# Two token-choice layers: product order, transposition banks, bias on TensorE, output stored by batch

## What is computed

```python
x = x + _L1_ffn_ref(_layernorm(x), router_w, router_b, expert_w, expert_b)

def _L1_ffn_ref(x, router_w, router_b, expert_w, expert_b):
    k = int(bs * C / NUM_EXPERTS)                 # 2048 / 16 = 128 tokens for each expert
    xf = x.reshape(bs, h)
    S = jax.nn.softmax(xf @ router_w + router_b, axis=-1)
    G, idx = jax.lax.top_k(S.T, k)                # each expert takes its 128 best tokens
    tokens = xf[idx]
    out = jnp.einsum('ekh,hd->ekd', tokens, expert_w) + expert_b
    weighted = G[..., None] * out
    y = jnp.zeros((bs, h)).at[idx.reshape(-1)].add(weighted.reshape(-1, h))
    return y.reshape(b, s, h)
```

## Time and profile before

| | us |
|---|---|
| median of 3 runs (lowest to highest) | 3072.86 (3069.28 to 3079.09) |
| the profiled execution, its own time | 3071.74 |
| its span in the profile | 3070.0 |
| PE busy | 2791.3 (91%) |
| DVE busy | 1616.8 (53%) |
| POOL busy | 996.4 (32%) |
| ACT busy | 844.4 (28%) |
| mean granted clock of PE, of full speed | 0.924 |

### The profile page before, as it was taken

How to read it: one execution, slowest core, us unless ns; L and a number is a source line. 1 busy time by engine, 2 the same in 40 slices (tenths; PEclk the granted TensorE clock), 3 DMA queues, 4 the chain that set the end, 5 groups by cost and what they waited for, 6 DMA issues and landing times. The chain is left out here.

```text
span 3070.0 us, 45793 instructions
## 1 busy us (share of the span) xinstructions
PE 2791.3 (91%) x15592; PEld 1943.7 (63%) x15592; DVE 1616.8 (53%) x4517; ACT 844.4 (28%) x1372; POOL 996.4 (32%) x1109
## 2 busy tenths in 40 slices
PE   7999999999999999999978999999999658888876
PEld 3434448887656556788867888888887533443444
DVE  4566645555655647455534333333344566555556
ACT  2343344443111101344432222222222002222210
POOL 0000027766544435577741122222221011212211
PEclk8999999999999999999989999999998558888875
DMA  3000020000000000200000000000000000000000
GB/s 142 1 0 0 0 103 1 0 0 0 1 0 0 0 0 0 83 0 0 0 14 1 15 15 15 15 1 15 15 1 1 24 0 1 1 1 0 1 0 28
DMA packets 6289, 37.96 MB, mean 12 GB/s; under 512 B 273, under 2 KB 4369, under 8 KB 4497
## 3 DMA queue, kind: packets, MB, share of 16 engines
q1 hardware_dynamic: 6160, 36.34, 3.0%
HBM read 34.24 MB, written 2.10 MB: 12 GB/s over the span
## 5 line engine op out<-in xcount | busy, mean ns | idle before, releaser
L603 PE MATMUL banks<-back 32*128 32x512 f32 (+3 forms) x1088 | 363.9, 599 | 31.5 <-DVE back L613 22.3
L365 PE MATMUL banks<-moe_parts 128*128 128x512 f32 x1536 | 366.9, 394 | 16.8 <-POOL moe_parts L471 10.3
L830 ACT ACTIVATE back<-banks 128x1024 f32<-128x1024 f32 (+3 forms) x256 | 217.1, 863 | 457.8 <-PE banks L724 457.5
L365 PEld LDWEIGHTS banks<-moe_parts 128*128 128x128 f32 x1536 | 286.2, 190 | 79.7 <-issue 22.4
L1449 PE MATMUL banks<-lin_parts 128*128 128x512 f32 x1152 | 309.1, 414 | 19.3 <-DVE lin_parts L1705 15.5
L1640 DVE TENSOR_TENSOR ffn_pack<-banks,back 128x512 f32<-128x512 f32 x128 | 88.5, 692 | 393.7 <-PE banks L1462 393.6
L1449 PEld LDWEIGHTS banks<-lin_parts 128*128 128x128 f32 x1152 | 213.2, 194 | 78.2 <-issue 31.2
L724 PE MATMUL banks<-back 32*128 32x512 f32 (+3 forms) x1024 | 239.4, 577 | 20.2 <-DVE back L846 12.8
L603 PEld LDWEIGHTS banks<-back 32*128 32x128 f32 x1088 | 134.2, 197 | 186.3 <-DVE back L617 77.9
L1770 POOL TENSOR_TENSOR ffn_pack<-ffn_pack 128x256 f32<-128x256 f32 x112 | 82.6, 738 | 456.9 <-ACT ffn_pack L1603 455.5
L617 DVE TENSOR_REDUCE back<-banks 128x1 f32<-128x512 f32 x272 | 176.5, 687 | 80.3 <-PE banks L603 75.6
(11 more groups left out here) (234 smaller groups left out, 5154.6 us busy)
## 6 DMA issues: line engine op xcount, KB each, us to landing
back<-p_raw SPq DMA_DIRECT2D x8, 1024.0 KB, 4.8
back<-p SPq DMA_DIRECT2D x1, 7696.0 KB, 21.2
ffn_pack<-ffn SPq DMA_DIRECT2D x1, 6144.0 KB, 26.8
back<-p SPq DMA_DIRECT2D x1, 5152.0 KB, 15.1
back<-p SPq DMA_DIRECT2D x2, 1792.0 KB, 8.2
out<-x SPq DMA_DIRECT2D x1, 2048.0 KB, 7.5
x<-x_in SPq DMA_DIRECT2D x1, 1536.0 KB, 12.7
small_pack<-small SPq DMA_DIRECT2D x1, 619.0 KB, 5.0
```

What stands on the lines that cost most here:

```text
L365: mm = nc.tensor.matmul(bank[:], up[:, n % 2, a, which, kd, :], xp[:, b, kd, :], start=((a, b, kd) == (0, 0, 0)), stop=((a, b, kd) == (1, ...
L603: nc.tensor.matmul(bank[:, 0:n], qs[head_rows[j], hg, qi * P:(qi + 1) * P], ks[head_rows[j], hg, 0:n], start=True, stop=True).then_inc(D.f ...
L830: nc.scalar.activation(pt[:, (kt % 2) * 2 + pair, :, q0:T], two[:, :, q0:T], ACT.Exp, scale=0.25).then_inc(A.free.s, 2)
```

## The change

The layer's order on PE becomes: router of batch 0; the four products of batch 0; transpositions of batches 1 and 2; router of batch 1; transposition of batch 3; products 4 and 5; routers of batches 2 and 3; products 6 and 7; then the transposed scores. The remaining eight products follow the first eight counts. Ring S gets a second pair of banks. ACT copies two banks of y before the transposed batches, and a third before the softmax. The expert bias, which POOL added, is written into a bank of y by a matmul of the identity with the broadcast bias (512 columns), on which the two products then accumulate. In the last layer DVE signals after each batch of x, and SP stores that batch with a DMA of its own; the last block only waits.

```diff
-    S.take([c.psum[2]])
+    S.take([c.psum[1], c.psum[2]])
...
+    EARLY = 2 * NT
+
     def after_count(u):
 
-        return range(0, 2) if u < 0 else range(u + 2, u + 3) if u + 2 < B * NT else ()
+        return range(EARLY + u, EARLY + u + 1) if EARLY + u < B * NT else ()
...
+                if i % 2 == 0:
+                    nc.tensor.matmul(bank[:].rearrange("p (a d) -> p a d", a=2), c.ident[:],
+                                     eb.unsqueeze(1).to_broadcast([P, 2, DM]), start=True, stop=False,
+                                     skip_group_check=True)
                 for kd in range(KD):
                     mm = nc.tensor.matmul(bank[:, (i % 2) * DM:(i % 2 + 1) * DM], xt_of[b][:, kd, i * P:(i + 1) * P],
-                                          ew[:, kd, :], start=(kd == 0), stop=(kd == KD - 1))
+                                          ew[:, kd, :], start=False, stop=(kd == KD - 1), skip_group_check=True)
...
             router(0)
-            for b in range(1, B):
-                turn(b)
-                router(b)
-            for n in after_count(-1):
+            for n in range(NT):
+                product(n)
+            turn(1)
+            turn(2)
+            router(1)
+            turn(3)
+            for n in range(NT, NT + 2):
+                product(n)
+            router(2)
+            router(3)
+            for n in range(NT + 2, EARLY):
                 product(n)
...
+            keep_y(0)
+            keep_y(1)
+            for b in range(1, B):
+                keep_turned(b)
+            keep_y(2)
             act.wait_ge(c.lg_ready.s, c.lg_ready.at(0, 1))
             nc.scalar.activation(tiles, tiles, ACT.Exp).then_inc(c.ex_ready.s, 1)
-            for n in range(B * NT // 2):
+            for n in range(3, B * NT // 2):
                 keep_y(n)
...
-            dve.wait_ge(c.y_ready.s, c.y_ready.at(0, B * NT // 2))
+            dve.wait_ge(O.free.s, O.released(0, "y", B - 1, 1))
             for b in range(B):
                 for i in range(NT):
                     n = b * NT + i
                     ins = nc.vector.scalar_tensor_tensor(out=c.x[:, b, i, :], in0=y[:, b, i, :],
                                                          scalar=co[:, n // 2, n % 2:n % 2 + 1],
                                                          in1=c.x[:, b, i, :], op0=ALU.mult, op1=ALU.add)
-            link(ins)
+                ins.then_inc(c.mixed.s, 1)
+            dve.wait_ge(c.mixed.s, c.mixed.at(0, B))
...
-        @block.gpsimd
-        def _(pool):
-            pool.wait_ge(c.s_small.s, 16)
-            for n in range(B * NT // 2):
-                b, h = n // 2, n % 2
-                pool.wait_ge(O.free.s, O.released(0, "y", b, h))
-                ys = y[:, b, 2 * h:2 * h + 2, :]
-                nc.gpsimd.tensor_tensor(ys, ys, eb.unsqueeze(1).to_broadcast([P, 2, DM]), ALU.add)\
-                    .then_inc(c.y_ready.s, 1)
...
+        def store(sp):
+            for b in range(B):
+                sp.wait_ge(c.mixed.s, c.mixed.at(0, b + 1))
+                sp.dma_start(out_dram[:, b], c.x[:, b]).then_inc(c.s_out.s, 16)
+
...
-            (ATTENTION, [(choice_layer, load_p7), (mla_layer, nothing), (choice_layer, nothing)]),
+            (ATTENTION, [(choice_layer, load_p7), (mla_layer, nothing), (choice_layer, store)]),
...
-                sp.dma_start(out_dram, c.x[:]).then_inc(c.s_out.s, 16)
-                sp.wait_ge(c.s_out.s, 16)
+                sp.wait_ge(c.s_out.s, 16 * B)
```

More of the change, by code:

```diff
@@ L1862, in choice_layer @@
     D.take(c.banks[0:2])
-    S.take([c.psum[2]])
+    S.take([c.psum[1], c.psum[2]])
     O.take(c.banks[6:8])
     D.open(B + 1 + STEPS + 2)
-    S.open(B - 1)
+    S.open(B - 1, whole=False)
     O.open(B * NT // 2)
@@ L1871, in choice_layer @@
     c.s_ready.open(1)
-    c.y_ready.open(B * NT // 2)
+    c.mixed.open(B)
     c.sum_ready.open(STEPS + 3)
-    c.ve.open(14 + 4 + 2 * STEPS - 1 + 1 + 5)
+    c.ve.open(14 + 4 + 2 * STEPS - 1 + 1 + 4)
     xt_of = [c.xt] + [xts[:, b] for b in range(B - 1)]
     xn_of = [None, c.xn, xn2, c.xn]
+    EARLY = 2 * NT
     def after_count(u):
-        return range(0, 2) if u < 0 else range(u + 2, u + 3) if u + 2 < B * NT else ()
+        return range(EARLY + u, EARLY + u + 1) if EARLY + u < B * NT else ()
     with nc.Block() as block:
@@ L1956, in _, with keep_turned @@
             nc.scalar.activation(warm, c.ident[:, 0:1], ACT.Exp)
-            for b in range(1, B):
+            def keep_turned(b):
                 act.wait_ge(S.full.s, S.may_read(0))
@@ L2081, in _ @@
             loads(sp)
-    for k in (D, S, O, c.xn_ready, c.lg_ready, c.ex_ready, c.s_ready, c.y_ready, c.sum_ready, c.ve):
+    for k in (D, S, O, c.xn_ready, c.lg_ready, c.ex_ready, c.s_ready, c.mixed, c.sum_ready, c.ve):
         k.close(1)
@@ L2297, in program @@
         c.s_ready = Count(sem("s_ready"))
-        c.y_ready = Count(sem("y_ready"))
+        c.mixed = Count(sem("batch_mixed"))
         n1, nf, n3, n5, n7 = (a.shape[1] for a in (p1, ffn, p3, p5, p7))
```

## The result

The changed kernel took 3035.04 us (median of 4 runs, 3029.85 to 3042.10), the kernel before 3071.07 beside it (4 runs): ratio 0.9897, 95% interval 0.9872 to 0.9923. The profiled spans are 3070.0 and 3039.6, 30.4 us apart; the mean granted clock went from 0.924 to 0.939.

What follows compares the result with a forecast made beforehand. In the two token-choice layers, 89.5 us each, the chain hardly leaves PE and DVE, with PE mostly at half clock. Per layer -7 + 1 - 4.5 = -10.5, twice -21, store -5: -26, giving 3046 us, range 3033 to 3059.

Steps and rivals of the forecast that it cites:

- Stretch A: Layer start to last router, 28.9 us before: filling PE's idle time and closing gaps gains 7 us; 8.2 at full clock.
- Stretch B: Last router to transposed scores, 4.6 us before: 0.7 us gained at full clock, 1.8 lost at half; 1 lost taken.
- Stretch C: Fifteen threshold steps, 43.8 us before: 4.9 us gained without POOL's additions, bias now on PE; 4.5 gained taken.
- Stretch D: Ties, coefficients and 16 additions to x, 12.1 us before: same instructions, so zero change.
- The store: Behind the last layer: four pieces, one after each four additions, gain 4.2 to 5.2 us; 5 taken.
- The sum: Whole program: 10.5 us gained per layer, 21 for two, 5 at the store, 26 in all.
- Half clock only in the steps: Rival, threshold steps: the clock stays down after the last two routers, gaining only 12 us, 3060; 13%.
- Half clock throughout: Rival, whole layer: PE's clock falls in batch 0's first bank and never returns, slower than before, 3087; 3%.
- Stores in series: Rival, program end: each piece starts only when the one before has landed, 2.6 us later than now, 3053 or 3054; 8%.
- L2034 not cured: Rival, threshold steps: the 0.86 us multiplication is long for a reason other than POOL, 4.9 us not gained, 3056; 3%.
- signs of being wrong: Clock 0.50 in the first 20 us; early steps of 4 us; stores landing 4 us apart; PE idle before a router.

Runs made afterwards that it cites:

- e6: The changed kernel without products before the last router, the rest behind the counts; layers 75.56 and 76.30 us, against 74.80 and 77.14 with the change.
- e2: The changed kernel with the expert bias back on POOL and no identity matmul on PE; layers 84.28 and 84.73 us.
- e7: The kernel before without POOL's bias additions and nothing in their place; layers 84.56 and 84.58 us, against 89.48 and 89.49 before.
- e3: The changed kernel with the single store of before; from the last addition to the end of the span 8.6 us instead of 3.4.
- e1: The kernel before with only the bias moved from POOL to PE through the identity; layers 84.80 and 84.96 us, against 89.48 and 89.49 before.

## Why the prediction was right, and where it was off

The time fell inside the range, and for the reasons given in the main; some sizes and one reason were off. That it lies inside owes something to luck too: the layers gained 6 us more than forecast, and 4.1 of that were given back where the prediction had put nothing.

**Stretch A.** Taken: 7 us. Worked out at full clock: 8.2. Measured: 8.5 and 7.8. The clock was full in the ladder but for the last routers, and the ladder took 11.84 where 11.4 were worked out. The term was set too low because I stepped down from the full-clock sum without a row for it. The reason, "this stretch now begins with 20 such passes", is not shown: e6 has none of them there and reaches A = 18.9 and 21.5. Nor was the clock up in them throughout: it was 0.50 over 2962 to 2964, and the two banks took 7.1 us where 5.4 were worked out, which just fits into the 7.26. And "DVE's normalisation, which starts the ladder at S + 9.3, is not touched" holds only because the bias leaves POOL in the same change: in e2 the early copies of y put POOL's additions into that normalisation, and A gained 2.3 to 2.8 instead of 8. I had priced POOL's leaving in the steps alone; it is the order's condition too.

**Stretch B.** Both of its cases came, one in each layer: -0.64 where -0.7 was worked out at full clock, +1.54 where +1.8 was at half. The +1 taken was meant for both.

**Stretch C.** The 7 x 0.70 = 4.9 were right to 0.01 us (e7). "One late count (1.6) before the clock is back, six steps shorter by 0.2" was right in kind and off in size: the late step took 3.49 and 2.91, 0.87 and 0.29 beyond 2.62, and eight and seven steps that had been longer were 2.42. (The 3.0 for fifteen such steps counted the first, which took 2.42 before.) Measured -5.5 and -6.0, taken -4.5.

**Stretch D** was 12.16 in both layers, as before: zero, as said.

**The store.** Taken 5, measured 5.2 (e3). The pieces did not follow each other: each lands 3.0 us after its issue, and the next is issued 1.6 us after it. By the Trainium skill's "SBUF — State Buffer", section "The DMA setup-cost knee", one large transfer was the better form; for a result that becomes ready piece by piece at the end of the program, the measured end (3.4 us behind the last addition, against 8.6) decides otherwise.

**The sum.** Layers: -21 forecast, -27.0 measured. The rest of the program was costed at nothing; it took 4.1 more in the latent attention and 2.2 less ahead of layer 1. The second is no effect of the change: that start lay between 2400.6 and 2413.2 in the fourteen profiles, of kernels that do the same up to there. Such a scatter is larger than any single term of the sum, which is why the experiments were read by stretches. By medians the gain is 36 us where 27 were forecast; the runs of either kernel differ by 12 us and more.

**The rivals.** Half clock only in the steps fell: 1.00 over 2996 to 2998, steps of 2.42. Half clock throughout fell: 1.00 in the ladder. Stores in series fell (3.0 us each, issued 1.6 apart). L2034 not cured fell: no such operation over 0.2 us. Of the signs of being wrong one did appear, a clock of 0.50 in the first 20 us: it cost nothing, since it lay in the time in which PE had idled and the ladder still began at S + 9.25.

## What to carry to other kernels

Take a side engine's work off its engine before moving producers earlier: an addition on POOL that had cost 0.7 us in a step fell into DVE's normalisation when its input came early, and took back 5 to 6 us of 8. Where PE waits and its clock halves, an order without gaps can be worth more than less work; but two edits that both close gaps need not add up, so test each without the other. A final store that follows the work piece by piece left only its last piece to wait for. And where a stage with a changing clock follows, measure a gain behind that stage.

## What was not expected of the hardware

- A POOL fill of 0.95 us that only writes doesn't hold DVE's two-input operation (0.16 us inside it); beside a POOL addition of 1.09 us such an operation took 0.86 to 0.95, and a one-input operation on 128x12 int32 (L164) 1.09.
- With 14 more passes of PE among a layer's counts, most steps took 2.42 us instead of 2.63 (e1 against e7).
- Two transposition groups in a row at half clock were followed by full clock in e6 (router 1.71), and in the last layer of e2 by 8 us more at half (router 3.23), with PE at work without a gap in both.
- A stage in which nothing was changed took between 470.2 and 477.3 us, and the distance between the two layers took five values about 3.4 us apart.
